# A relational graph layer on one Trainium2 core: where TensorE loads two register values, and in which order SyncE issues two DMA transposes

## What is computed

```python
h = relu(layernorm(x))
S = h[src]                                        # one row per edge
msg = relu(relu(S @ W_rel[r].T + b_rel[r]) @ W_rel[r].T + b_rel[r])   # r: the edge's relation
agg = segment_sum(msg, dst)                       # per node
i, f, g, o = split(agg @ W_ih.T + b_ih + b_hh)
hn = sigmoid(o) * tanh(sigmoid(i) * tanh(g))
out = x + W3(relu(W2(relu(W1 hn))))               # with the biases b1, b2, b3
```

## Time and profile before

| what | us |
|---|---|
| median of 3 runs (2488.23 to 2498.43) | 2492.32 |
| the profiled execution's own time | 2501.18 |
| its span, first to last instruction | 2499.5 |
| TensorE busy (matmuls) | 2152.1 (86%) |
| VectorE busy | 1792.3 (72%) |
| ScalarE busy | 1634.5 (65%) |
| GpSimd busy | 1165.0 (47%) |

### The profile page before, as it was taken

One profiled execution on the slowest core, in us unless ns is written; L12 is line 12 of the kernel. 1 busy time (PEld: TensorE's weight loads), 2 busy tenths in 40 slices (PEclk: granted clock), 3 DMA queues, 4 the chain that ended last, 5 costly groups with the idle time before them and its releaser, 6 DMA issues.

```text
span 2499.5 us, 51857 instructions
## 1 busy us (share of the span) xinstructions
PE 2152.1 (86%) x14224; PEld 1410.9 (56%) x14225; DVE 1792.3 (72%) x4311; ACT 1634.5 (65%) x3366; POOL 1165.0 (47%) x917
## 2 busy tenths in 40 slices
PE   6858676758998989989998989989898999899996
PEld 5747555635555556655555555556555566444443
DVE  7546555546777777777787777777777777678885
ACT  2547555537777777777777777677776777566663
POOL 0047777774554555555555555555545543300000
PEclk7569999879999999999999999999999999999998
DMA  9935555566778888887888888888878887887885
GB/s 388 425 124 101 93 96 95 98 106 112 143 148 152 155 158 159 155 150 144 158 161 150 151 150 157 159 160 157 150 144 158 157 159 140 165 185 174 191 188 137
DMA packets 400606, 396.90 MB, mean 159 GB/s; under 512 B 263738, under 2 KB 343158, under 8 KB 394360
## 3 DMA queue, kind: packets, MB, share of 16 engines
q0 software_dynamic: 91200, 157.34, 40.1%
q1 hardware_dynamic: 306788, 238.12, 36.6%
q10 hardware_dynamic: 2516, 0.14, 0.1%
HBM read 185.88 MB, written 156.97 MB: 137 GB/s over the span
## 4 chain that ended last, share of the span: by engine, by line
PE 52%; issue 16%; DMA 11%; ACT 9%; POOL 5%; SPq 4%; DVE 2%; another core or an unknown queue 0%; POOLq 0%; ACTq 0%; DVEq 0%
PE bank L1472 25%; PE bank L1419 6%; PE bank L1486 4%; DMA a_lo<-row_lo 4%; DMA agg<-summed,scatter_idx 3%; DMA y<-in_x 3%; PE bank L1455 3%; PE bank L1438 3%; PE bank L1511 3%; PE bank L1401 3%; POOL xg L667 3%; POOL agg L655 2%; SPq L605 2%; PE bank L1311 2%; ACT summed L727 1%
## 5 line engine op out<-in xcount | busy, mean ns | idle before, releaser
L655 POOL DMA_INDIRECT agg<-summed,scatter_idx x400 | 637.0, 1593 | 754.7 <-DVE scatter_idx L1147 565.3
L1472 PE MATMUL bank<-a_hi,ihT 128*128 128x512 f16 x2400 | 725.3, 384 | 27.6 <-DMA a_lo<-row_lo 26.4
L667 POOL DMA_INDIRECT xg<-in_x,src_ring x400 | 429.2, 1073 | 268.9 <-DMA src_ring<-src_slot 138.0
L1472 PE MATMUL bank<-a_lo,ihT 128*128 128x512 f16 x1200 | 460.4, 384 | 0.0
L1472 PEld LDWEIGHTS bank<-a_hi,ihT 128*128 128x128 f16 x2400 | 233.8, 99 | 252.4 <-issue 49.7
L1438 PE MATMUL bank<-relT,h_hi 128*128 x1600 | 325.0, 277 | 0.0
L1401 PE MATMUL bank<-ident,xn 128*128 128x128 f32 x800 | 132.4, 290 | 210.9 <-issue 112.7
L1419 PE MATMUL bank<-s_hi,relT 128*128 128x256 f16 x1600 | 300.6, 284 | 0.0
L733 ACT ACTIVATE s_hi<-bank 128x512 f16<-128x512 f32 x200 | 119.7, 599 | 210.0 <-PE bank L1401 185.7
L780 ACT ACTIVATE g_i<-bank,gate_b 128x512 f32<-128x512 f32 x200 | 137.5, 687 | 180.2 <-PE bank L1472 179.0
L1073 DVE SCALAR_TENSOR_TENSOR s_lo<-bank,s_hi 128x512 f16<-128x512 f32 x200 | 137.5, 688 | 159.6 <-ACT s_hi L733 120.1
(11 more groups left out here) (197 smaller groups left out, 4732.7 us busy)
## 6 DMA issues: line engine op xcount, KB each, us to landing
agg_in<-agg SPq DMA_DIRECT2D x100, 512.0 KB
y<-in_x POOLq DMA_DIRECT2D x100, 512.0 KB
out<-y SPq DMA_DIRECT2D x100, 512.0 KB
agg<-zeros SPq DMA_DIRECT2D x24, 2112.0 KB, 15.8
dst_ring<-dst_rows SPq DMA_DIRECT2D x200, 128.0 KB
xg<-in_x,src_ring POOLq DMA_INDIRECT x400
agg<-summed,scatter_idx POOLq DMA_INDIRECT x400
src_ring<-src_slot SPq DMA_DIRECT2D x200, 1.0 KB
```

Source lines behind the costliest of these rows:

```text
L655: nc.gpsimd.indirect_dma_start(out=agg[:, :], out_offset=bass.IndirectOffsetOnAxis(ap=scatter_idx[:, k.slot(8), t:t + 1], axis=0), in_=sum ...
L667: nc.gpsimd.indirect_dma_start(out=xg[:, k.slot(8), t, :], out_offset=None, in_=x[:, :], in_offset=bass.IndirectOffsetOnAxis(ap=src_ring[: ...
L1472: last = nc.tensor.matmul(N_C[c % 2][:, 0:UNIT], lhs, rhs, start=i == 0, stop=i == len(todo) - 1)
```

## The change

On TensorE `relations(at)` moves: in a shared step from the head of the step to behind the second chunk, in an edge step to behind the transposes. On SyncE the turn for unit + 1 moves from the end of a step to right behind `dst_ring`, ahead of the load of `agg_in` and the store of `y`.

```diff
 # SyncE, step(at)
                 (dst_ring's load)
+                k = at.unit + 1
+                if k.within(UNITS):
+                    if not at.odd:
+                        sp.wait_ge(row_hi_ready, k.n + 1)
+                        sp.sem_inc(row_hi_cleared, 1)
+                        wait_from(sp, chunk_done, (k.n - 1) * CHUNKS)
+                        sp.sem_inc(row_hi_cleared, 1)
+                        sp.dma_start_transpose(a_hi[...], row_hi[...])
+                    else:
+                        sp.wait_ge(row_ready, k.n + 1)
+                        sp.sem_inc(row_cleared, 1)
+                        sp.dma_start_transpose(a_lo[...], row_lo[...])
                 if not at.odd:
                     (agg_in's load for unit + 2, y's store of unit - 4)
-                (the same turn for unit + 1 as above)
 # TensorE
             def edge_step(at):
+                turn_s(at)
                 rel_of = relations(at)
-                turn_s(at)
                 layer_h(at - 1, rel_of.get(1))
             def both_step(at):
                 k, half = at.unit, at.odd
-                rel_of = relations(at)
                 turn_s(at)
                 chunk(k, 3 * half)
                 chunk(k, 3 * half + 1)
+                rel_of = relations(at)
                 layer_h(at - 1, rel_of.get(1))
```

More of the change, by code:

```diff
@@ L573, in step @@
                                  ).then_inc(dst_loaded[k.slot(2)], 16)
+                k = at.unit + 1
[5 more added lines that the diff above has]
+                        sp.sem_inc(row_hi_cleared, 1)
+                        sp.dma_start_transpose(a_hi[:, k.slot(2), :, :, :].rearrange("p t h n -> p (t h) n"),
+                                               row_hi[:, k.slot(2), :, :].rearrange("p t d -> p (t d)")
+                                               ).then_inc(a_hi_turned[k.slot(2)], 16)
+                    else:
+                        sp.wait_ge(row_ready, k.n + 1)
+                        sp.sem_inc(row_cleared, 1)
+                        sp.dma_start_transpose(a_lo[:, k.slot(2), :, :, :].rearrange("p t h n -> p (t h) n"),
+                                               row_lo[:, k.slot(2), :, :].rearrange("p t d -> p (t d)")
+                                               ).then_inc(a_lo_turned[k.slot(2)], 16)
                 if not at.odd:
@@ L596, in step @@
                                      y[0:UR, k.slot(Y_SLOTS), :, :]).then_inc(stored[k.slot(Y_SLOTS)], 16)
[L597 to L613, removed]
             run_steps(sp, -10, last=LAST, step=step, **RUN)
```

## The result

| what | before | after |
|---|---|---|
| median of 20 runs each, same chip | 2491.82 (2486.74 to 2501.50) | 2502.31 (2492.53 to 2517.74) |
| the profiled execution's own time | 2501.18 | 2493.03 |

The ratio is 1.0039, 95% interval 1.0020 to 1.0057: the change costs 10 us (5 to 14), under the 0.5% that I called no change, but on the other side from the 20 us forecast. The time is within the range given (2425 to 2530). A ratio compares executions taken side by side and leaves out those more than 1.5% above their kernel's fastest (seven of the twelve of e3, none elsewhere), so it need not be the quotient of two medians.

The account below looks back on a forecast made before the run. TensorE was taken as the bound in the shared and last stages, with idle time at the register load. Shared stage -114 us plus last stage +94 made -20 us, so a median of 2472 us, range 2425 to 2530.

Parts of the forecast that it names:

- Register load, shared stage: TensorE, before the transposes: two chunks cover the register load, so all 126 us of idle time go.
- The wait for `a_lo` in the shared stage: Before chunk 0: lateness averages 0.35 us a unit, 25 us in all, +11.5 us against today's 13.5.
- the nearest row is the 4.34: Flight of `a_lo`, shared stage: a 4.34 us row set against 4.27 us of room, giving 0.35 us a unit.
- The 5.12 us: Shared stage: time from issue of `a_lo` to chunk 0 when nothing was late; less 0.85 it gave 4.27 us room.
- Rival A: Shared stage, chunk 0: `a_lo` late by 1 us on average, net +26 us, 2518; chance 0.18.
- a shared unit above 20.7: Sign of a wrong direction: a shared unit staying above 20.7 us, where 20.4 was forecast.
- The last stage: SyncE: load and store between the turns cost 3.7 us a unit, 89 us over 24 units; a unit takes 15.
- Rival D: Last stage: the nearer store lengthens the turn's flight by 2.25 us, 147 us lost, net +33, 2525; chance 0.12.
- the rule on the flight: DMA queue, last stage: `a_lo` can't be seen before the store and load ahead of it are done.
- Rival C: TensorE, shared stage: the register load is not covered and nothing is gained, 2576; chance 0.05.
- Rival B: Last stage costs only 48 us, as an `a_lo` turn alone issues in 1.26 us: net -66, 2426; chance 0.15.
- The edge stage: TensorE, edge steps: no gain or loss, 0 us, since the `xn` it waits for is not moved.

Follow-up runs that it names:

- e3: Changed kernel with the turn of `row_lo` right behind that of `row_hi` in the even step, ahead of load and store, all stages: 2503.07 us, ratio 1.0007.
- e9: The kernel before, unchanged, profiled a second time: 2465.31 us, ratio 0.9991.
- e4: The changed kernel, unaltered, profiled a second time: 2484.81 us, ratio 1.0034 to the kernel before.
- e10: e6 with the store of `y` moved to the odd step behind the turn of `row_lo`, shared steps only: 2312.97 us, ratio 0.9378.
- e8: Changed kernel with `relations(at)` behind the first chunk instead of the second: 2494.90 us, ratio 1.0005 to the kernel before.
- e5: Changed kernel with SyncE's old order (load, store, then the turns) in the last stage only: 2412.19 us, ratio 0.9687 to the kernel before.
- e1: The kernel before with the TensorE part of the change only: 2442.18 us, ratio 0.9853.
- e2: The kernel before with the SyncE part of the change only: 2586.57 us, ratio 1.0431.
- e7: Changed kernel with the store of `y` moved to the odd step behind the turn of `row_lo`, all stages: 2410.78 us, ratio 0.9674.
- e6: e5 with the turn of `row_lo` ahead of the load of `dst_ring` in odd shared steps: 2371.39 us, ratio 0.9509.
- e11: e6 with TensorE's register load back at the head of the step, ahead of the transposes, in the edge stage: ratio 0.9536.

## Why the prediction was wrong

**The account.** us, forecast against the profiled executions, and against the second traces (e9, e4; they are of two chips, so the line ahead of unit 0 is taken from e9 and e10):

| stretch | forecast | first pair | second pair |
|---|---|---|---|
| ahead of unit 0 | 0 | -9.5 | -4.6 |
| shared stage | -114 | -85.0 | -73.6 |
| units 71 to 75 | +5 | +5.9 | +5.1 |
| last stage | +89 | +83.4 | +77.8 |
| rest | 0 | -3.0 | -1.0 |
| sum | -20 | -8.2 | +3.7 |

The medians have +10.5 and +8.4 (e4's ratio). The second pair is 5 to 7 us under them; no trace of both kernels from one chip, both at their median, is there, and this rest stays open.

**Register load, shared stage: right.** 126 us of idle time were to go and went: no "issue" before L1401, none before L1412; e8 shows margin beyond that. e9 to e10 closes the account on one chip: the issue waits (109.1 us, 142 times, so 109.1 + 142 x 0.16 = 131.8) and the `a_lo` waits (14.1 to 1.4, 12.7 us) make 144.5, of 151.8 measured; the remaining 7 us fit what 13.7 us at half the clock cost in e9 (none in e10).

**The wait for `a_lo` in the shared stage: the step that failed.** The mechanism was right, its size was not. I forecast 0.35 us a unit, 25 us in all, and so +11.5 against today's wait. It was 1.0 us a unit, 66 us over 66 units (e4: 66.7, e5: 67.0), which is 48 to 53 more than before and 52 to 57 over the 71 units. The shared stage gave 74 us by the second pair instead of 114; these 40 us are more than the 30 between the forecast and the result. Two sizes were off, both in "the nearest row is the 4.34".
- Flight: 4.54 us by the median (4.35 in e4), not 4.34 as an upper end. In the kernel before it was 4.01 (3.82 in e9). Neither part of the change alone lengthens it (e1 3.87, e2 3.99). Together they put the store about 3.0 us ahead of the turn, where it was 4.5, and taking it out from there (e7) gives 3.94 at the same room. Within the trace after it is the same: the flight is 4.92 us by the median in the 18 units with the store less than 2.6 us ahead, 4.72 in the 35 with 2.6 to 3.7, and 3.70 in the 4 with over 5 (e4: 4.72, 4.55 and 3.74). So in this order of the queue the store does it. It is no general rule: in e1 the flight is 3.63 in the 16 units with the store as near as 2.6 to 3.7 us, and in what way the store slows the turn no run shows.
- Room: 4.01 us by the median and 3.84 in the mean, not 4.27. The turn stands behind `dst_ring`, which waits for `same` from VectorE (L1124), and VectorE lags in steps of its own; e6 takes that dependency away and the room goes to 5.49.

From one row without a wait and one with a wait I took a value near the better one, without a term for what lies between. The 5.12 us was a good case: over units 4 to 69 of the trace of before the median room was 4.06 us and the median flight 4.01. Unit by unit the median slack was 0.23 us, and 22 of the 66 turns had none; after the change 57 had none.

**Rival A was what happened.** It said that `a_lo` would be late by 1 us on average and that the whole decides at a gain of 1.3 us a shared unit. The lateness was 1.0 us, the gain 1.2 (first pair) or 1.04 (21.90 to 20.86), below that point. Its sum was 26 us lost against 10 measured, because the last stage with the units before it cost 83 to 89 and not 94, the shared stage gained 74 to 85 and not 68, and the edge stage gained some. I had its place and its price right and gave it 18 of 100. My sign for being wrong in direction, "a shared unit above 20.7", was met at 20.83.

**The last stage: right in mechanism, a little too large.** Forecast 15.0 us a unit and 3.7 us lost; measured 14.76 and 14.48, 3.47 and 3.24 lost. The turn came 2.9 us later behind its sibling (3.1 forecast; 2.8 by the median), the wait was 3.0 to 3.2 us (2.9), the clock's fall cost up to 0.64 us (0.8): nine stretches of 3.4 us in 24 units, half of 30.7 us. e5 gives all of it back.

**Rival D and the rule on the flight.** In the last stage the store is now 0.49 us ahead of the turn, not 2.7. If the increment of `a_lo` had to wait for the whole store, it would have grown by up to 2.25 us; it grew from 4.48 to 4.87 by the median (4.60 in e4). The store lands 4.24 us after its issue, `a_lo` 5.33 us after that of the store, and in all 24 units later than it. So this trace agrees with the order that the Trainium skill (DMA: Bandwidth & Descriptors, "Queues, rings and completion order") gives, since the earlier write does land first. It does not test it: the store was done 3.8 us (3.5 in e4) after the issue of the turn, before the 4.30 us that the turn takes in e7 with no store close ahead, so there was nothing to hold back. The nearer store cost 0.3 (e4) to 0.6 us of flight, by a way that stays open.

**Rival C** fell (e8). **Rival B** fell in the size: the `a_lo` turn did take 1.4 us to issue, not 2.2, but the flight did not shrink with it (4.60 to 4.87 us against 4.48).

**The edge stage: the 0 was wrong, by 4 us.** It was argued that what TensorE waits for (`xn`) is not moved. But `xn` depends on TensorE in turn, as its wait halves when the transposes come earlier (e10 against e11). Which buffer or engine closes that ring was not traced. In steps 0 to 12 the order costs 5 us or more, for a reason that stays open.

## What to carry to other kernels

A sequencer's own work (a register load, bound checks) costs nothing behind a few matmuls and 0.9 us a step at a place where the engine has just run dry; move it, but expect the next releaser, here a DMA transpose whose median slack was a quarter of a us, to take back more than a third of the gain. Take the slack of what is late next from the distribution over all units, not from two rows. And an order in a DMA-issuing queue is good for one stage only: the order that helped nothing in the shared stage by itself cost nearly 80 us in the last, where load and store had filled a wait. Choose it per stage, with the transfer that the bound engine needs ahead of everything that can wait (0.938 instead of 1.004).

## What was not expected of the hardware

- Two DMA transposes 1.4 us apart flew 7.2 and 12.2 us, and beside them the waits for gathers and scatters of another queue came to 361 and 399 us (e3, one long execution); 4.2 us apart (e10), 4.5 and 6.75 us, with 74 us of waits for gathered rows and 12.9 us for scatters (48.1 and 6.0 in the trace after).
- With a store of 512 KB ahead of it a DMA transpose flew 0.3 to 0.6 us longer in the last stage (0.47 us ahead) and 0.4 to 0.6 us in the shared stage (about 3 us ahead), e4 and the trace after against e7.
- Pauses of about 3 us on TensorE cost clock at once in 8 of 24 cases only (5 in e4), and the low stretch (3.4 us at 1.2 GHz) then begins at or up to 1.2 us after the next matmul.
